# Softmax of a score tile: one maximum, one shift and one exp for all sixteen heads, in place of a split of twelve heads and four

## The reference

```python
# cross attention: 16 heads of 16, queries from layernorm(x), keys and values from ctx
Q = split_heads(layernorm(x) @ Wq.T + bq);  K = split_heads(ctx @ Wk.T + bk);  V = split_heads(ctx @ Wv.T + bv)
energy = einsum('bhqd,bhkd->bhqk', Q, K) / sqrt(16)
energy = where(mask[:, None, None, :] == 0, -1e10, energy)
attention = softmax(energy, axis=-1)
x = x + tanh(g_xattn) * (einsum('bhqk,bhkd->bhqd', attention, V) merged @ Wfc.T + bfc)
# experts: the best 2 of 8 for each token
logits = layernorm(x) @ gate;  w = softmax(top2(logits))
x = x + tanh(g_ffn) * sum over the 2 chosen experts n of w_n * ((silu(h @ w0[n]) * (h @ w1[n])) @ wo[n]),  h = layernorm(x)
```

## Time and profile before

| | |
|---|---|
| median of three runs | 1369.81 us (1364.96, 1369.81, 1369.87) |
| the profiled execution | 1363.92 us, its span 1362.3 us |
| first stage | about 24 to 683 us of the span |
| second stage | about 684 us to the end |
| busy share of the span | PE 93%, PE weight load 81%, DVE 55%, ACT 51%, POOL 55% |
| granted clock of PE, mean | 0.962 of full speed |

### The profile page before, as it was taken

How to read it: one execution, slowest core, us unless ns; L and a number is a source line. 1 busy time by engine, 2 the same in 40 slices (tenths; PEclk the granted TensorE clock), 3 DMA queues, 4 the chain that set the end, 5 groups by cost and what they waited for, 6 DMA issues and landing times.

```text
span 1362.3 us, 37316 instructions
## 1 busy us (share of the span) xinstructions
PE 1263.6 (93%) x10466; PEld 1109.6 (81%) x10467; DVE 746.4 (55%) x2524; ACT 699.2 (51%) x1780; POOL 750.6 (55%) x1197
## 2 busy tenths in 40 slices
PE   4999999999999999997099999999999999999996
PEld 3888888888888888886078888888888888888885
DVE  5788788877888878873333333333333333333332
ACT  2777677767777777774033333333333333333332
POOL 3367777776777767775434444444444444444443
PEclk9999899989999999996589999999999999999998
DMA  5034333323334333326468863333333333333332
GB/s 157 23 119 138 132 126 123 127 74 116 128 124 136 132 126 128 124 100 218 150 186 213 218 146 53 54 54 54 53 52 53 54 54 54 54 54 50 57 53 34
DMA packets 73976, 139.73 MB, mean 103 GB/s; under 512 B 11604, under 2 KB 55156, under 8 KB 71764
## 3 DMA queue, kind: packets, MB, share of 16 engines
q0 software_dynamic: 32064, 52.46, 19.7%
q1 hardware_dynamic: 39840, 86.05, 19.5%
q10 hardware_dynamic: 2036, 0.75, 0.2%
HBM read 68.95 MB, written 70.27 MB: 102 GB/s over the span
## 4 chain that ended last, share of the span: by engine, by line
PE 49%; issue 1%; DMA 0%; POOL 0%; POOLq 0%; ACT 0%
PE banks L1424 28%; PE psB L1443 14%; PE psT L1432 4%; PE psG L1409 2%; DMA out_dram<-ey,eid 0%; POOL w_part L500 0%; DMA et<-routed_rows 0%; POOL routed_rows L494 0%; POOL out_dram L551 0%; POOLq L545 0%; ACT ey L774 0%; ACT etT L756 0%; POOLq L546 0%; POOLq L306 0%; POOLq L559 0%
## 5 line engine op out<-in xcount | busy, mean ns | idle before, releaser
L1424 PE MATMUL banks<-w_all,etT 128*128 x1620 | 433.3, 403 | 0.7 <-ACT etT L756 0.7
L1424 PEld LDWEIGHTS banks<-w_all,etT 128*128 128x128 f32 x1620 | 286.3, 189 | 51.4 <-issue 3.6
L1151 DVE TENSOR_TENSOR hgT<-psT,hgT 128x512 fp32r<-128x512 f32 x135 | 93.3, 691 | 426.0 <-ACT hgT L768 426.0
L551 POOL DMA_INDIRECT out_dram<-ey,eid x135 | 216.5, 1604 | 91.4 <-issue 48.0
L546 POOL DMA_DIRECT2D et<-routed_rows x135 | 76.8, 569 | 300.6 <-issue 233.0
L1443 PEld LDWEIGHTS psB<-w_all,hgT 128*128 128x128 f32 x1620 | 208.5, 188 | 18.8 <-issue 1.3
L1443 PE MATMUL psB<-w_all,hgT 128*128 x1620 | 218.5, 284 | 0.8 <-ACT hgT L768 0.8
L774 ACT ACTIVATE ey<-psB,ewt 128x256 f32<-128x256 f32 x135 | 64.2, 475 | 234.1 <-PE psB L1443 143.8
L1279 PEld LDWEIGHTS psB<-vbd,probT 128*128 128x128 f32 x1280 | 163.1, 194 | 21.9 <-ACT probT L622 20.1
L1279 PE MATMUL psB<-vbd,probT 128*128 128x51 f32 x1280 | 168.0, 271 | 13.4 <-ACT probT L622 13.4
L762 ACT ACTIVATE hs<-banks 128x512 f32<-128x512 f32 x135 | 80.7, 598 | 185.3 <-PE psT L1432 183.4
(11 more groups left out here) (162 smaller groups left out, 2188.6 us busy)
## 6 DMA issues: line engine op xcount, KB each, us to landing
split_weights<-w_part SPq DMA_DIRECT2D x16, 1536.0 KB, 6.2
w_all<-split_weights SPq DMA_DIRECT2D x32, 768.0 KB, 4.7
et<-routed_rows POOLq DMA_DIRECT2D x135, 129.0 KB, 2.4
xb<-in_x_dram SPq DMA_DIRECT2D x32, 256.0 KB, 2.8
w_raw<-in_L_ffn_w_kernel_dram SPq DMA_DIRECT2D x32, 256.0 KB
out_dram<-x SPq DMA_DIRECT2D x64, 128.0 KB
w_raw<-in_L_ffn_wo_kernel_dram SPq DMA_DIRECT2D x16, 256.0 KB
cb<-in_ctx_dram SPq DMA_DIRECT2D x32, 77.0 KB
```

What stands on the lines that cost most here:

```text
L551: gp.indirect_dma_start(out=out, out_offset=bass.IndirectOffsetOnAxis(ap=eid[:, u:u + 1], axis=0), in_=ey[:, u % 2, :], in_offset=None, co ...
L1151: dve.tensor_tensor(hgT[:, 1].rearrange("p c q -> p (c q)"), psT[:], hgT[:, 0].rearrange("p c q -> p (c q)").bitcast(F32), ALU.subtract).t ...
L1424: m = pe.matmul(banks4[:, bank], etT[:, u % 2, a, c], weight(e, c, w, n), start=(j == 0), stop=(j == len(steps) - 1))
```

## The change

All sixteen heads take the path of the first twelve. DVE does one maximum over 128x1232 scores and one shift over 128x1232; ACT does one exp over 128x1232 of `prob`. Gone are the maximum of four heads, `s_negate` with its tile `neg_mx`, the four exps with a bias, and the semaphores `s_neg` and `s_heads`. The one maximum stands where the maximum of twelve stood.

```diff
             def exp_scores(i, t):
-                act.wait_ge(s_neg, i + 1)
-                for j, h in enumerate(range(S_FULL * HB, H)):
-                    act.activation(prob[:, t, h * K2:(h + 1) * K2], psS[:, S_FULL, j * K2:(j + 1) * K2], ACT.Exp,
-                                   bias=neg_mx[:, t, j:j + 1], scale=scale).then_inc(s_heads, 1)
                 act.wait_ge(s_sub, i + 1)
-                shifted = prob[:, t, 0:S_FULL * HB * K2]
-                act.activation(shifted, shifted, ACT.Exp, scale=scale).then_inc(p_done, 1)
+                act.activation(prob[:, t, 0:HK], prob[:, t, 0:HK], ACT.Exp, scale=scale).then_inc(p_done, 1)
...
-            def s_largest(i, t, part):
+            def s_largest(i, t):
                 dve.wait_ge(s_ps, RG * (i + 1))
-                sv, h0, n, k = S_PARTS[part]
-                dve.tensor_reduce(mx[:, t, h0:h0 + n * k].rearrange("p (n h) -> p n h", n=n), sv, AX_X, ALU.max).then_inc(s_max, 1)
-
-            def s_negate(i, t):
-
-                dve.wait_ge(s_max, 2 * i + 1)
-                dve.tensor_scalar(neg_mx[:, t], mx[:, t, S_FULL * HB:H], -scale, None, ALU.mult).then_inc(s_neg, 1)
+                dve.tensor_reduce(mx[:, t].rearrange("p (n h) -> p n h", n=RG), S_ALL, AX_X, ALU.max).then_inc(s_max, 1)
 
             def s_shift(i, t):
-                dve.wait_ge(s_max, 2 * (i + 1))
+                dve.wait_ge(s_max, i + 1)
...
                     if softmax:
-                        s_largest(i + 1, 1 - t, 1)
                     if known(i, 2):
                         stats_2(i - 2, t, 1)
                     if keys:
                         k_evac(b + 1)
                     if values:
                         v_split(b + 1, 0)
-                    if softmax:
-                        s_negate(i + 1, 1 - t)
                     if chosen_now:
                         choose(i - 3, 1 - t, 0)
                     if softmax:
-                        s_largest(i + 1, 1 - t, 0)
+                        s_largest(i + 1, 1 - t)
...
                 if known(i, 1):
                     pe.wait_ge(s_sub, i)
-                    pe.wait_ge(s_heads, HB * i)
```

More of the change, by code:

```diff
@@ L43, in flamingo_gated_layer @@
     S_BANKS = [(n, h, HB) for n, h in enumerate(range(0, H, HB))]
-    S_FULL = RG - 1
     PAIR = HP * K2
@@ L156, in flamingo_gated_layer @@
         mx = sb("mx", [P, 2, H])
-        neg_mx = sb("neg_mx", [P, 2, H - S_FULL * HB])
         rden = sb("rden", [P, H])
@@ L245, in flamingo_gated_layer @@
         s_ps, s_max, s_sub, p_done = sem("s_ps"), sem("s_max"), sem("s_sub"), sem("p_done")
-        s_neg, s_heads = sem("s_neg"), sem("s_heads")
         t_ps, t_sb, o_ps, o_rec, o_sb = sem("t_ps"), sem("t_sb"), sem("o_ps"), sem("o_rec"), sem("o_sb")
@@ L905, in v_evac @@
                                   head_of[:].rearrange("p c (h o) -> p (c h) o", o=1).to_broadcast([P, CH * 3, HD]), ALU.mult).then_inc(v_sb, 1)
-            split = S_FULL * HB
-            S_PARTS = [(psS[:, 0:S_FULL, 0:HB * K2].rearrange("p n (h k) -> p n h k", k=K2), 0, S_FULL, HB),
-                       (psS[:, S_FULL:S_FULL + 1, 0:(H - split) * K2].rearrange("p n (h k) -> p n h k", k=K2), split, 1, H - split)]
-            def s_largest(i, t, part):
+            S_ALL = psS[:, 0:RG, 0:HB * K2].rearrange("p n (h k) -> p n h k", k=K2)
+            def s_largest(i, t):
                 dve.wait_ge(s_ps, RG * (i + 1))
-                sv, h0, n, k = S_PARTS[part]
-                dve.tensor_reduce(mx[:, t, h0:h0 + n * k].rearrange("p (n h) -> p n h", n=n), sv, AX_X, ALU.max).then_inc(s_max, 1)
-            def s_negate(i, t):
-                dve.wait_ge(s_max, 2 * i + 1)
-                dve.tensor_scalar(neg_mx[:, t], mx[:, t, S_FULL * HB:H], -scale, None, ALU.mult).then_inc(s_neg, 1)
+                dve.tensor_reduce(mx[:, t].rearrange("p (n h) -> p n h", n=RG), S_ALL, AX_X, ALU.max).then_inc(s_max, 1)
             def s_shift(i, t):
-                dve.wait_ge(s_max, 2 * (i + 1))
-                sv, h0, n, k = S_PARTS[0]
-                dve.tensor_tensor(prob[:, t, h0 * K2:(h0 + n * k) * K2].rearrange("p (n h k) -> p n h k", n=n, k=K2), sv,
-                                  mx[:, t, h0:h0 + n * k].rearrange("p (n h o) -> p n h o", n=n, o=1).to_broadcast([P, n, k, K2]),
+                dve.wait_ge(s_max, i + 1)
+                dve.tensor_tensor(prob[:, t, 0:HK].rearrange("p (n h k) -> p n h k", n=RG, k=K2), S_ALL,
+                                  mx[:, t].rearrange("p (n h o) -> p n h o", n=RG, o=1).to_broadcast([P, RG, HB, K2]),
                                   ALU.subtract).then_inc(s_sub, 1)
@@ L1012, in _ @@
             late_constants()
-            s_largest(0, 0, 1)
-            s_negate(0, 0)
-            s_largest(0, 0, 0)
+            s_largest(0, 0)
             s_shift(0, 0)
```

## The result

The changed kernel took 1327.48 us (median of four runs, 1325.61 to 1334.16) against 1367.67 us for the kernel before beside it. The ratio is 0.9716, with a 95% interval of 0.9674 to 0.9757: 2.8% less time, where the prediction had 0.66% and a range that began at 1350. The direction was right and the size missed by a factor of four.

A forecast was written before the change was run, and what follows sets the result against it. The prediction took a loop through five engines' queues, 18.49 us a pair, as the bound. 0.34 - 0.04 = 0.30 a pair, times 28 = 8.4, plus 0.6 elsewhere: 9.0 off the median 1369.81 gives 1360.8 us; range 1350 to 1370.

The forecast's parts named there:

- That closes a loop: First stage: waits through the engines' queues, DVE to POOL (by `slot`) to ACT to PE to DVE, make the 18.49 us pair.
- mv* ahead of the scores: count 0: t = 1 tile: POOL's 28 waits for `mv`, 38.8 us in total, shorten, but PE waits longer in t = 0: 0.
- Maxima and shift, 0.34 us a pair: DVE, t = 1 tile, on the loop: merged maximum saves 0.65 us, longer shift costs 0.31.
- Exps, hidden: ACT: one exp in place of five saves 0.58 us a tile, hidden because PE reads the result 0.69 us later: 0.
- Negation in the t = 0 tile: DVE's L921, 0.75 us, goes, but that tile's softmax is not on the loop: 0.
- The price of two engines in each other's way: DVE and POOL blocking each other: between 0.08 us a pair gained and 0.31 lost; 0.04 lost was taken.
- at 0.15 only: Argument against the first rival (all given back, chance 0.22): DVE's and POOL's bursts already met in one pair of two, costing 0.15.
- PE's waits count in full: Rival, chance 0.04: the loop is misread and the t = 1 tile's 0.4 us is gained too, 11 us more: 1350.
- Fewer drops of the clock: Rival, chance 0.12: PE's waits in t = 1 tiles go, its clock stays up, up to 10 us more come off: 1351.
- What it named as proof against itself: Signs that would prove the prediction wrong: a pair shorter by 0.6 us or more, or POOL's stretch grown by over 0.2.
- then another loop was the limit: What the prediction said would follow if the pair were shorter by 0.6 us or more.

The follow-up runs named there:

- e1_mv_first: Kernel before, with only DVE's instruction that makes `mv` moved ahead of the maximum of four; softmax still split: 1329.15 us, ratio 0.9739.
- e6_mv_waits_for_scores: Changed kernel, with DVE waiting for the scores before it makes `mv` in t = 1 tiles, nothing moved: 1359.94 us, ratio 0.9944.
- e5: Changed kernel, with the one maximum ahead of the key evacuation and the value split, `mv` still first: 1331.26 us, ratio 0.9746.
- e2: Split softmax of the kernel before, with DVE's queue in the changed kernel's order: 1348.23 us, ratio 0.9863.
- e11: Changed kernel, with the instruction that writes `slot` moved behind `o_norm(i, 1)`, about 1.1 us later: 1346.09 us, ratio 0.9842.
- e4: Changed kernel, with the instruction that writes `slot` moved to the end of DVE's tile, about 1.9 us later: 1386.44 us, ratio 1.0164.
- e8: e5 with both parts of the first layernorm's statistics (`mv1`) ahead of `q_low` in t = 0 tiles: 1328.55 us, ratio 0.972.
- e10: e8 with the maximum ahead of the keys in t = 0 tiles only, and two of POOL's copies a pair done by DVE: 1325.72 us, ratio 0.9703.
- e7: Changed kernel, with `mv` behind the one maximum in t = 1 tiles only: 1437.32 us, ratio 1.0514.
- e3: Changed kernel, with `mv` right behind the one maximum in both kinds of tile: 1482.35 us, ratio 1.0867.

## Why the prediction was wrong

- **"That closes a loop"**: the step that failed. Its links from POOL to ACT to PE and back to the scores are right. Their sum is the period, but that shows nothing: any chain from one maximum of four to that of the next pair adds up to 18.49, whichever links it is cut into. The link from DVE to POOL was the wrong one. The prediction took the 0.82 us ahead of the first scatter as a wait for `slot`, since the profile named it. The same 0.84 is there after, with `slot` unwritten; and the code has that scatter take the `slot` of the tile before. The link is `mv`: scores, maximum of four, `mv`, then POOL's L466, and in the pair of the earlier trace rows no further wait of POOL for DVE.
- **"*mv* ahead of the scores: count 0"**: the term that carried the result. 38.8 us of waits in 28 pairs stood in the earlier trace rows, and this was dismissed because `slot` was thought to hold the loop, and PE was to wait that much longer in the t = 0 tile. That wait did not grow: 0.48 us before, 0.39 to 0.41 after. With the right link the wait for `mv` is on the loop in full: POOL's wait was 0.88 to 0.96 us where the clock stayed up, and 0.96 a pair was measured. e1_mv_first makes this shown, not argued; e6_mv_waits_for_scores undoes most of it with one wait.
- **Maxima and shift, 0.34 us a pair**: the durations were right to 0.03 us, but were not on the loop. e1, which keeps them as they were, is as fast within the intervals. `slot` did come 0.3 us sooner after the maximum's start, as forecast, and nothing waited for it.
- **Exps, hidden**: right. ACT's 0.6 us a tile bring nothing by themselves, as e1 and e5 show. **Negation in the t = 0 tile, nothing**: right for the order of before; in the changed kernel's order the merging matters there (e2, 1348), in part through where DVE and POOL meet.
- **The price of two engines in each other's way**: not a term of the result, but its bound of 0.31 was too small, and so was "at 0.15 only". The prediction read L467 and L887. In the kernel before, in every other t = 0 tile, this stood as well (timelines of DVE and of POOL):

```profile
397.25 1.23 DVE L976 TENSOR_TENSOR chosen<-expert_f,topf 128x16 f32<-128x16 f32 x1
```

```profile
397.18 1.27 POOL L500 TENSOR_TENSOR w_part<-w_raw,w_part 128x512 fp32r<-128x512 f32 x1
```

  In the changed kernel's regular pairs that product takes 0.16 us. This isn't where the gain comes from: in e6_mv_waits_for_scores that product never takes over 0.65 us between 150 and 550 us, and the time is 1360. In e2 and e11 such meetings did cost time.
- **Rivals**: "PE's waits count in full", with a chance of 0.04, was nearest: it said that the t = 1 gain counts too. "Fewer drops of the clock", 0.12, also came true: some 8 of the 33.7 us. Both at once, about 1340, lay outside the range, which was made as if the cases excluded each other; and even that is 12 us over the result, since 0.3 + 0.4 a pair is less than the 0.96 measured.
- **What it named as proof against itself** held: the pair is shorter by over 0.6, "then another loop was the limit".

What now limits isn't settled to one link. POOL's queue has no wait in pairs with two weight splits, POOL waits 1.28 us for `mv1` in the others, `slot` binds when it is 1 to 2 us later, and three edits that relieve one or two of these stay at 1326 to 1329 us, with POOL waiting for `mv` in place of `mv1`.

## What to carry to other kernels

In an in-order queue, price an edit first by what it lets past a wait, then by the instructions that it saves: here one 0.2 us instruction, moved ahead of a wait for another engine, was worth 2.6%. When a loop is built from the profile's releasers, check each link against the code's semaphore and its count; a wait with the same length in every turn, ending just after the named one, may be a start delay. And a clock that falls with waits makes both signs larger: add it to the other cases, rather than keep it as a case apart.

## What the runs showed of the hardware

The first indirect DMA of a pair started 0.82 to 0.85 us after what it needed, in all thirteen traces, and one that waited for DVE's `slot` likewise (0.84 in e4); one with nothing to wait for followed 0.3 us behind the one before. So a wait of this length, named after another engine, need not be a wait for it.

Small instructions of DVE (2 to 16 elements, 0.16 us) took 1.23 to 1.25 us when they started just after a weight split of POOL, and ended with it: in the kernel before, e2 and e11.

PE's granted clock from 150 to 550 us went with how PE waited: 1.00 in the changed kernel, e1, e5 and e8 to e10, 0.98 in e2, 0.97 in the kernel before, e6 and e11, 0.93 in e4, 0.88 in e7 and 0.85 in e3. A wait of 0.4 to 0.5 us in each t = 0 tile left it at full speed in the changed kernel; in e7, where PE also stood 1.26 us in t = 1 tiles, it was at half speed (1.2 GHz) about a quarter of the time. That is why 1.8 us more a pair cost 110 us and not 51.
